# GpSimd clears 240 unread columns between every two indirect transfers of a fused attention and mixture-of-experts layer

## What is computed

```python
score = relu(xf @ rw1 + rb1) @ rw2 + rb2
_, topi = top_k(score, 2)                      # 8 experts, two for each token
gate = softmax(where(mask, score, -inf))
for e in range(8):
    h = relu(xf @ W1[e] + b1[e])               # 128 -> 512
    y = h @ W2[e] + b2[e]                      # 512 -> 128
    out = out + gate[:, e:e + 1] * y
x = x + gb * out
```

## Time and profile before

| | |
|---|---|
| median of 3 runs | 565.93 us (563.48 to 565.95) |
| profiled execution, its own time | 570.48 us |
| its span from first to last instruction | 568.7 us |
| mean granted TensorE clock | 0.904 |
| TensorE busy | 449.6 us (79%) |
| VectorE busy | 376.0 us (66%) |
| ScalarE busy | 347.1 us (61%) |
| GpSimd busy | 321.0 us (56%) |
| indirect transfers, lines 1612 and 1645 | 64 of 980 ns and 72 of 990 ns |

### The profile page before, as it was taken

The page is one execution under the profiler, slowest core; times in us unless marked ns, Lnnn a source line. Parts: engine busy times, 40 slices in busy tenths (PEclk is TensorE's granted clock), DMA queues, the critical chain, the costliest instruction groups (busy, mean ns, idle before and its releaser), DMA issues.

```text
span 568.7 us, 16627 instructions
## 1 busy us (share of the span) xinstructions
PE 449.6 (79%) x5323; PEld 354.7 (62%) x5323; DVE 376.0 (66%) x1026; ACT 347.1 (61%) x1521; POOL 321.0 (56%) x458
## 2 busy tenths in 40 slices
PE   6997988888888888879295925369415999999977
PEld 5565666656666666655052415369314999999977
DVE  6768999999999999984851522265114545555574
ACT  3769999999999999895133512034002758755720
POOL 6976555556886687545373375501773445445450
PEclk9999999999999999999686875678755999999989
DMA  8341000000003003022112011202221222222547
GB/s 224 114 144 28 14 12 13 12 14 13 14 12 104 13 12 87 14 79 55 42 53 63 29 61 47 67 17 54 81 70 55 67 75 74 74 75 72 180 114 221
DMA packets 61518, 36.53 MB, mean 64 GB/s; under 512 B 25806, under 2 KB 57334, under 8 KB 61306
## 3 DMA queue, kind: packets, MB, share of 16 engines
q1 hardware_dynamic: 55834, 25.83, 17.0%
q0 software_dynamic: 4352, 9.45, 4.9%
q10 hardware_dynamic: 1248, 0.20, 0.2%
HBM read 20.56 MB, written 14.88 MB: 62 GB/s over the span
## 4 chain that ended last, share of the span: by engine, by line
PE 35%; ACT 21%; DVE 19%; issue 11%; another core or an unknown queue 11%; POOL 2%; DVEq 1%; ACTq 0%; POOLq 0%
ACT pr L1026 19%; PE pAm L1920 10%; DVE nmax L1093 7%; PE pSpm L1928 5%; PE pScm L1928 5%; PE pAm L1483 5%; PE pScm L1253 2%; DVE oT L947 1%; PE pScm L1498 1%; PE pm L767 1%; DVE stat L1335 1%; POOL hn L351 1%; PE pSpm L1490 1%; PE pXm L1912 1%
## 5 line engine op out<-in xcount | busy, mean ns | idle before, releaser
L1026 ACT ACTIVATE pr<-pS,nmax 128x136 f32<-128x136 f32 x512 | 184.9, 380 | 13.5 <-DVE nmax L1093 13.3
L1685 ACT ACTIVATE act<-pAm,w1t 128x128 f32<-128x128 f32 x288 | 82.2, 389 | 103.1 <-remote 49.8
L1026 ACT ACTIVATION_READ_ACCUMULATOR pr<-pS,nmax 128x1 f32 x512 | 108.6, 212 | 0.0
L1645 POOL DMA_INDIRECT y_scr<-ys,si x72 | 71.3, 990 | 65.3 <-DVE ys L1794 46.2
L1920 PE MATMUL pAm<-hgT,w1t 128*128 128x128 f32 x576 | 85.1, 292 | 16.4 <-DVE w1t L1778 8.1
L1055 PE MATMUL pS<-kT,qbd 64*128 64x136 f32 x1024 | 93.9, 302 | 1.5 <-ACT pr L1026 1.2
L1093 DVE TENSOR_REDUCE nmax<-pS 128x4 f32<-128x544 f32 x128 | 87.6, 685 | 2.1 <-PE pS L1059 1.4
L1920 PEld LDWEIGHTS pAm<-hgT,w1t 128*128 128x128 f32 x576 | 77.3, 207 | 17.3 <-issue 11.4
L1101 DVE STREAM_TRANSPOSE prT<-pr 128x640 f32<-128x640 f32 x96 | 81.1, 845 | 8.7 <-ACT pr L1026 0.2
L1055 PEld LDWEIGHTS pS<-kT,qbd 64*128 64x128 f32 x1024 | 68.3, 186 | 14.5 <-ACT pr L1026 1.1
L1612 POOL DMA_INDIRECT xs<-h_all,pos_i x64 | 62.7, 980 | 19.5 <-issue 18.0
(11 more groups left out here) (303 smaller groups left out, 695.3 us busy)
## 6 DMA issues: line engine op xcount, KB each, us to landing
hg<-xs SPq DMA_DIRECT2D x72, 72.0 KB
vbd<-v_scr SPq DMA_DIRECT2D x132, 16.0 KB, 1.7
v_scr<-h_all SPq DMA_DIRECT2D x8, 256.0 KB, 2.3
h_all<-y_scr SPq DMA_DIRECT2D x8, 256.0 KB
w_all<-y_scr SPq DMA_DIRECT2D x8, 256.0 KB, 5.4
x_all<-in_L_attn_x SPq DMA_DIRECT2D x3, 512.0 KB, 6.0
w_all<-in_L_ffn_W SPq DMA_DIRECT2D x2, 768.0 KB, 4.8
w_all<-in_L_ffn_W SPq DMA_DIRECT2D x3, 512.0 KB, 5.4
```

Of the source, the lines that this page charges most:

```text
L1026: e.activation(pr[:, n, to:to + SPAN], scored(j, gi)[:, lo:lo + SPAN], ACT.Exp, bias=nmax[:, k:k + 1], scale=-1.0, accum_out=rs[u][:, k:k ...
L1645: e.indirect_dma_start(out=y_scr, out_offset=bass.IndirectOffsetOnAxis(ap=si[:, j:j + 1].bitcast(U32), axis=0), in_=ys[j % R // 2][:, j % ...
L1685: e.activation(ac(u)[:, k, :], pU[u % W][:, k, :], ACT.Relu, bias=w1t[u // 2 % 4][:, u % 2, FF + D + k:FF + D + k + 1]).then_inc(a_up.sem, 1)
```

## The change

Behind each dispatch, and behind each scatter but the last eight, GpSimd clears the 240 columns of a new tile `unread`, which nothing reads. Each clear raises a semaphore, and the next clear waits for it.

```diff
@@ -1182,6 +1182,8 @@
             ys = [sm(f"ys{u}", [P, 2, D]) for u in range(RP)]
             si = sm("si", [P, NF], I32)
+            unread = sm("unread", [P, 240])
+            p_br = sem("m_p_br")
             gated = sm("gated", [P, NT // 2, 2, P])
@@ -1645,16 +1647,29 @@
                                          in_=ys[j % R // 2][:, j % 2, :], in_offset=None).then_inc(d_y[j % R // 2], 16)
 
+                breaths = [0]
+
+                def breath():
+
+                    if breaths[0]:
+                        e.wait_ge(p_br, breaths[0])
+                    e.memset(unread[:, :], 0.0).then_inc(p_br, 1)
+                    breaths[0] += 1
+
                 sent = 0
                 for p, (first, end) in enumerate(PARTS):
                     routed(e, p)
                     for r in range(2 * first, 2 * end):
                         dispatch(e, r // 2, r % 2)
+                        breath()
                         if p == len(PARTS) - 1 and r % 2 == 1:
                             scatter(sent)
+                            breath()
                             sent += 1
                 for j in range(sent, NF):
                     scatter(j)
+                    if j < NF - 8:
+                        breath()
```

## The result

The changed kernel takes 539.21 us in the median of four executions against 565.11 before. One of the four took 805.22 us and is left out of the ratio; the median of the other three is 538.34, ratio 0.953 (95% interval 0.9486 to 0.9574). The forecast was 519 with a range of 500 to 562.

What follows compares the result with a forecast made beforehand. Closely spaced GpSimd transfers were taken to cause 58.1 us of dead time; spacing at 1.63 makes GpSimd the bound, last scatter 504.1 plus 17.9 tail, span 522.0, execution 523.8, less 4.55 for the median: 519, range 500 to 562.

Steps and rivals of the forecast that it cites:

- What bounds the kernel: Between 296 and 430 us, TensorE, VectorE and ScalarE stall while GpSimd sends transfers 1.27 us apart; 58.1 us of the chain.
- the six pieces of the earlier trace: Chain waits on "another core or an unknown queue" between 296 and 430 us: 4.16, 4.27, 12.63, 9.64, 23.35, 4.05 us.
- Theory B: Follow-up expectation: how long GpSimd sends, not transfer distance, sets dead time; 545 to 555 us expected with 480 columns.
- distance is not the cause: Rival, chance 0.15: engines stop for as long as GpSimd sends, so wider spacing lengthens the dead time; 593 us.
- up to 9 or 10 transfers at 1.27 are harmless: Reading of GpSimd's bursts: dead time starts 10.1 to 11.5 us into a burst; 16 such transfers are too many.
- the fourth burst: GpSimd's 28 dispatches and result scatters from 395.26 to 429.92 us, where the hardware queue is busy too.
- The price of one: One clear between GpSimd transfers raises the distance between starts from 1.27 to 1.63 us.
- my bounds of 1.34 and 2.10: Transfer distance in us: 1.34 if the clear hides beside the gap's preparation, 2.10 if each transfer pays a 0.76 wait.
- What GpSimd's line costs: Last scatter on GpSimd starts at 295.5 + 128 x distance: 504.1 us at 1.63, against 550.81 before.
- What the dead time gives back: If all dead time goes, the TensorE, VectorE and ScalarE chain is 58.1 us shorter; last scatter could start at 492.7.
- the first rival: Dead time stays where load is heaviest, in the last burst of dispatches and scatters: 545 us, chance 0.22.
- The lock: VectorE copies of the first matrix and GpSimd clears may hold each other up; 37 us at most, none taken on the path.

Runs made afterwards that it cites:

- groups one and two: Two sets of four follow-up kernels, each set on a chip of its own; the kernel before the change took 566.64 us on one, 563.78 on the other.
- the repeat: The changed kernel with 240 columns measured once more, unaltered: 537.31 us, ratio 0.9519 to the kernel before the change.
- 48 clears only: The changed kernel with 240-column clears behind the first 48 dispatches only, none from the last part on: 542.89 us, ratio 0.9621.
- pads late: The changed kernel with SP's eight writes of padding rows moved from list tile 23 to 39, behind the last dispatches: 536.33 us, ratio 0.9493.
- the thin kernel: The kernel before the change, with dispatches and list loads of 16 of 144 columns per row, experts working on zeros: 503.61 us, ratio 1.001.

## Why the prediction was right, and where it was off

**What bounds the kernel.** Right on the chips of the first measurement and of groups one and two: the six pieces of the earlier trace rows go as soon as the transfers are far enough apart (360, 480 and 720 columns have none over 1 us). Theory B and the rival "distance is not the cause" (593) fall: at 60 columns nothing changes, at 360 the total falls by 38.4. The reading "up to 9 or 10 transfers at 1.27 are harmless" was wrong: with a pause behind every eighth, the dead piece begins between the fourth transfer and the fifth.

By the Trainium skill (DMA: Bandwidth & Descriptors, Queues, rings and completion order) each transfer engine takes turns between its queues. By that rule spacing should give nothing; it gave 38.4 us on the second chip, so the turns of the transfer engines are not all that matters here, and the traces do not show what else does.

One candidate that the forecast did not name can be looked up in the trace before, for the fourth burst: that the engines wait for their next instructions to be loaded. TensorE's matmuls ahead of the end of the slow stretch and at it, and all that the DMA queues moved from 396.4 to 436.9 (packets, MB, share):

```profile
424.26 0.37 PE L1928 MATMUL pSpm<-w_all,act 128*128 x1 [1.73 <-issue]
...
434.77 0.46 PE L1912 MATMUL pTm<-ident,hg 128*128 128x128 f32 x1 [1.04 <-issue]
435.03 1.28 PE L1920 MATMUL pAm<-hgT,w1t 128*128 128x128 f32 x5
```

```profile
q0 software_dynamic: 896, 1.97, 14.6%
q1 hardware_dynamic: 1584, 0.81, 7.1%
```

The two queues that the page marks as "instruction" (q8, q14) moved nothing in that time, and TensorE was back at five matmuls in 1.28 us before they did. So this stretch did not end with an instruction load. The rows also show that TensorE crawls in it more than it stands: from 402 to 424 one or two matmuls start every 1.4 to 2.1 us, each behind idle time marked "issue".

**The price of one.** This step failed: 1.63 was forecast, 1.45 measured (1.54 with the clears and transfers that are held up, means 1.01 + 0.36 + 0.17). The 0.28 us behind the cast contains a wait for a semaphore; a transfer behind a clear whose result it does not wait for starts after 0.17. The case lies between my bounds of 1.34 and 2.10.

**What GpSimd's line costs.** The formula, last scatter = 295.5 + 128 x D with D from the measured means, was right wherever GpSimd is the bound: 505.4 against 506.0 (360 columns), 295.5 + 128 x 1.78 = 523.3 against 522.7 (480), 546 against 545.2 (720). With 240 columns it gives 295.5 + 128 x 1.54 = 492.6, and the measured 517.3 shows that GpSimd is not the bound.

**What the dead time gives back.** "If all of it goes" failed for the fourth burst. The pieces of the chain tell only part of it, since a stretch in which TensorE crawls can be "issue" in the chain. The start of the fortieth copy of the first matrix on VectorE, before, after, in the repeat and with 360 columns, shows how far each kernel has come:

```profile
477.14 0.50 DVE L1778 COPY w1t<-w_all 128x644 f32 x1 [0.39 <-DVE ys L1794]
...
443.51 0.57 DVE L1793 COPY w1t<-w_all 128x644 f32 x1 [0.39 <-DVE ys L1809]
...
443.72 0.50 DVE L1793 COPY w1t<-w_all 128x644 f32 x1 [0.39 <-issue]
...
412.20 0.53 DVE L1793 COPY w1t<-w_all 128x644 f32 x1 [0.39 <-issue]
```

In us, beside the dead pieces over 1 us between 284 and 440:

| kernel | first dispatch to the last part's first | from there to the fortieth copy | dead pieces |
|---|---|---|---|
| before | 110.6 | 81.9 | 59.6 |
| 60 columns | 107.5 | 81.5 | 23.6 |
| 48 clears only | 83.3 | 81.4 | 10.3 |
| 240 columns (the result) | 82.8 | 76.0 | 28.1 |
| 240 columns, repeat | 80.8 | 77.8 | 11.8 |
| 240 columns, pads late | 83.2 | 77.9 | 36.7 |
| 360 columns | 80.4 | 47.3 | 0 |

Ahead of the fourth burst 240 columns bring 27.8 us, nearly all that 360 bring (30.2). In the fourth burst they bring 5.9 of 34.6. That is the first rival, priced at 545, though at a distance of 1.45 and not at the 1.63 at which it was priced. At the distance that I had assumed, 360 columns, the dead time does all go, and 525.4 is measured where I had 519; 1.2 us of the difference is the longer tail (19.1 in place of 17.9), 1.9 the later last scatter (506.0 for 504.1), and 3.0 that I took the median 4.55 us below the profiled run, where here it is 1.51 below. The result lies within the range because two errors met: the clear was cheaper than forecast, and the shorter distance was too short for the fourth burst.

**The lock.** For 240 columns, where GpSimd is not the bound, its size is small as forecast: the copies' mean rises from 536 to 561 ns, 72 x 25 ns = 1.8 us; whether any of that is on the path is not shown. The clears pay too: 312 ns alone, up to 606, and all 25 that last over 0.34 us run beside a copy of line 1793. "Nothing on the path" fails where GpSimd is the bound. With 360 columns the clears take 417 ns in the median and 462 in the mean (busy us, mean ns, idle us before):

```profile
L1656 POOL MEMSET unread<- 128x360 f32 x128 | 59.2, 462 | 0.1
```

All 28 that last over 0.44 us run beside such a copy, and 128 x 0.045 = 5.8 us is my estimate of what they add to GpSimd's line. By the Trainium skill (SBUF — State Buffer, Who interferes with whom) a VectorE copy in a 2-port mode and a GpSimd instruction exclude each other for a whole instruction; the trace agrees in that both rows become longer where they meet, but it does not show the mode of the copy.

**What the forecast left out** is that the dead time seems to depend on the chip. Where it seems absent the kernel before stands at 502, close to 565.9 - 58.1 = 508, my price of the chain without it. A run with 240 columns there was not made; by the formula its last scatter would be near 493 where the thin kernel has 481.9, so my estimate is some 10 us slower than before.

## What to carry to other kernels

When a chain rests on waits that no instruction of the core explains, lay them beside the timeline of the engine that goes on working; here they stood in and just behind rows of closely spaced indirect transfers, and a distance of 1.62 us in place of 1.27 was worth 38 us. Do not take the sum of those waits for the time lost; compare when the kernels reach the same instruction. Sweep the delay and expect a narrow best: below it nothing is gained, above it GpSimd becomes the bound at 128 times the distance, and the two ends cost the same 566. And measure on more than one chip before keeping such a delay: on one of the chips here 300 columns cost 17 us.

## What the runs showed of the hardware that was not expected

- One kernel took 564 to 567 us on three occasions and 502.37 on another chip, 11% apart, with 13 runs from 500.44 to 503.0 on the last. That the dead pieces are the difference is argued, not shown.
- Indirect transfers of 128 rows at 1.27 to 1.30 us from start to start, eight or more in a row, left TensorE, VectorE and ScalarE standing or crawling on the chips of groups one and two; with starts 1.45 us apart the first three bursts were mostly free and the fourth was not, and at 1.62 on average and above all four were; a pause of 1.8 us ended the dead time within 0.5 to 1.6 us in six of nine pieces. What is short is open, and so is whether executions without a profiler show it: all times here come with recorded spans.
- A GpSimd clear starts without a gap behind an indirect transfer, and the next transfer 0.17 us behind the clear, though two transfers in a row have 0.30 between them.
